# Merged and reordered stack loads, and joint maxima of two heads, in a two-layer decoder kernel

## The reference, cut to what matters

```python
x = _layernorm(x + L0_attn(x))            # a0: causal self-attention
x = _layernorm(x + L0_xattn(x, ctx))      # c0: cross-attention, 512 queries, 1024 keys
x = _layernorm(x + L0_ffn(x))             # soft mixture: 8 experts, 128 slots each
x = _layernorm(x + L1_attn(x))            # a1: causal
x = _layernorm(x + L1_xattn(x, ctx))      # c1: cross
x = _layernorm(x + L1_ffn(x))             # a2: pre-norm causal attention, then top-2 of 8 experts

# one attention, per batch and head:
att = softmax(q @ k.T / sqrt(16))         # causal layers mask the upper triangle
y   = att @ v                             # then an output projection
```

## Time and profile before

| | before |
|---|---|
| median of 3 runs | 3067.17 us (3059.79 to 3073.33) |
| the profiled execution | 3064.33 us |
| its span, first to last instruction | 3062.5 us |
| PE / DVE / ACT / POOL busy | 84% / 49% / 44% / 15% of the span |
| mean granted clock of PE | 0.916 of full speed |

### The profile page before, as it was taken

One profiled execution on the slowest core, in us unless ns is written; L12 is line 12 of the kernel. 1 busy time (PEld: TensorE's weight loads), 2 busy tenths in 40 slices (PEclk: granted clock), 3 DMA queues, 4 the chain that ended last, 5 costly groups with the idle time before them and its releaser, 6 DMA issues. The chain is left out here.

```text
span 3062.5 us, 48054 instructions
## 1 busy us (share of the span) xinstructions
PE 2568.9 (84%) x15793; PEld 1469.9 (48%) x15794; DVE 1499.4 (49%) x4196; ACT 1346.1 (44%) x2886; POOL 457.8 (15%) x719
## 2 busy tenths in 40 slices
PE   4999999999828979998588999898987986489992
PEld 2555544444314446676355544343434554356671
DVE  0555677888425420013444487777744564222223
ACT  2555456666634432211244456665754553022220
POOL 3222212101110000000112212212122000500004
PEclk7899999999969999999699999999998997599996
DMA  8344664454000012203644465354422332711102
GB/s 205 97 126 126 131 118 82 68 73 73 1 17 1 1 59 88 87 17 137 158 109 123 111 128 80 56 101 62 92 59 60 103 83 95 249 31 34 34 30 89
DMA packets 184550, 259.98 MB, mean 85 GB/s; under 512 B 32952, under 2 KB 106944, under 8 KB 184256
## 3 DMA queue, kind: packets, MB, share of 16 engines
q1 hardware_dynamic: 181264, 248.85, 34.5%
q0 software_dynamic: 3072, 8.39, 0.9%
HBM read 180.71 MB, written 81.53 MB: 86 GB/s over the span
## 5 line engine op out<-in xcount | busy, mean ns | idle before, releaser
L1345 ACT ACTIVATE second_p<-psum 128x512 f32<-128x512 f32 (+3 forms) x1024 | 461.7, 520 | 287.9 <-PE psum L1211 284.3
L1345 ACT ACTIVATE first_p<-psum 128x512 f32<-128x512 f32 (+3 forms) x768 | 365.7, 547 | 179.1 <-PE psum L1211 176.5
L1419 DVE TENSOR_REDUCE first_max_parts<-psum 128x1 f32<-128x512 f32 x512 | 323.0, 684 | 74.7 <-PE psum L1188 72.1
L1419 DVE TENSOR_REDUCE second_max_parts<-psum 128x1 f32<-128x512 f32 x512 | 321.9, 683 | 72.9 <-PE psum L1188 70.2
L1415 DVE CUSTOM_DVE_ANT_0 second_masked<-psum,mask_qk 128x384 f32<-128x384 f32 (+3 forms) x512 | 230.0, 489 | 230.7 <-PE psum L1188 189.1
L1201 PE MATMUL psum<-second_q,second_k 64*128 64x512 f32 (+3 forms) x1024 | 227.7, 440 | 42.1 <-DVE second_max_parts L1419 26.2
L1188 PE MATMUL psum<-second_k,second_q 64*128 64x512 f32 (+3 forms) x1024 | 203.7, 395 | 67.5 <-DMA second_k<-a_k_parts 51.5
L1223 PE MATMUL psum<-second_p,second_v_aug 128*32 128x512 f32 (+3 forms) x2048 | 240.1, 542 | 8.3 <-ACT second_p L1345 8.1
L1188 PE MATMUL psum<-first_k,first_q 64*128 64x512 f32 (+3 forms) x768 | 158.0, 411 | 61.7 <-ACT first_held L1382 26.0
L1201 PEld LDWEIGHTS psum<-second_q,second_k 64*128 64x128 f32 x1024 | 98.8, 188 | 230.1 <-issue 83.6
L1415 DVE CUSTOM_DVE_ANT_0 first_masked<-psum,mask_qk 128x128 f32<-128x128 f32 (+3 forms) x256 | 114.8, 488 | 179.7 <-PE psum L1188 152.5
(11 more groups left out here) (317 smaller groups left out, 3819.2 us busy)
## 6 DMA issues: line engine op xcount, KB each, us to landing
first_k<-c_k_parts SPq DMA_DIRECT2D x128, 128.0 KB, 5.7
second_q<-a_q_parts SPq DMA_DIRECT2D x256, 64.0 KB, 2.8
second_k<-a_k_parts SPq DMA_DIRECT2D x256, 64.0 KB, 2.9
second_k<-c_k_parts SPq DMA_DIRECT2D x128, 128.0 KB, 5.6
first_q<-a_q_parts SPq DMA_DIRECT2D x128, 64.0 KB, 2.9
first_k<-a_k_parts SPq DMA_DIRECT2D x128, 64.0 KB, 2.9
c_k_parts<-first_held SPq DMA_DIRECT2D x16, 512.0 KB, 3.2
first_q<-c_q_parts SPq DMA_DIRECT2D x128, 64.0 KB, 5.3
```

Source lines behind the costliest of these rows:

```text
L1345: evacuated(act.activation(probs[tile % 2][:, 2 * h + p, q0:SEQ], bank[:, q0:SEQ], ACT.Exp, scale=scale), event)
L1419: evacuated(v.reduce_max(max_parts[n % 2][:, h, p, qt, k0 // BANK:k0 // BANK + 1], bank[:, 0:width], axis=AX_X), event)
```

## The change

It has four parts.

**Loads.** A stack's q and k come in 8 transfers in place of 16. One transfer fills 32 partitions: for q the same 16 rows twice (a broadcast of the source), for k both parts. On the host the columns of the q and k weights are reordered (`by_heads`) so that the two pairs' rows of one `d` lie next to each other, and one row of a transfer is 2 x 512 (or 2 x 1024) numbers in one piece. In a causal layer the k rows now fill the first 1024 columns of the buffer, which `keys_of` unpacks.

**Order of the first loads.** The weights of later layers become an event of the list, behind the first stacks' loads. In the first stage a0's own weights still go ahead of everything; in the second stage, whose first projections are made elsewhere, all weights are in the event. The first two contexts are fetched some steps later, and the first stage's four first loads stand between its pieces.

**Maxima.** The shared banks become 0 to 6 and the sum's bank 7. In a cross layer, where a unit's two heads have neighbouring banks, one `reduce_max` over both writes two columns; where the ring wraps between them, two single ones stay.

**Experts.** `w_in` becomes `up_in` (first weight and its bias) and `down_in` (second weight and its bias); PE and ACT begin on the first, DVE and PE's second half wait for the second.

```diff
-SHARED_BANKS, PV_BANK = (0, 1, 2, 3, 4, 5, 7), 6
+SHARED_BANKS, PV_BANK = tuple(range(7)), 7
...
+        def keys_of(n):
+
+            keys = layer_of(n).keys
+            return ks[n % NB][:, :, :].rearrange("p i t -> p (i t)")[:, 0:2 * keys].rearrange("p (i t) -> p i t", i=2)
+
...
-                for dst, src, columns in own_loads:
-                    sp.dma_start(dst, src, allow_slow_non_contiguous=columns).then_inc(own_in, 16)
-                for dst, src, columns in later_loads:
-                    sp.dma_start(dst, src, allow_slow_non_contiguous=columns).then_inc(later_in, 16)
+                def fetch_weights(loads, done):
+                    for dst, src, columns in loads:
+                        sp.dma_start(dst, src, allow_slow_non_contiguous=columns).then_inc(done, 16)
+
+                if not layers[0].projected:
+                    fetch_weights(own_loads, own_in)
...
-                        for blk, (qp, kp) in enumerate(((0, 0), (0, 1), (1, 0), (1, 1))):
-                            at = slice(64 * h + HD * blk, 64 * h + HD * (blk + 1))
-                            sp.dma_start(qs[n % NB][at, :, :].bitcast(F32),
-                                         q_dram[qp, row:row + 2 * HD, :].rearrange("(i d) t -> d i t", d=HD)
+                        for half in range(2):
+                            at = slice(64 * h + 2 * HD * half, 64 * h + 2 * HD * (half + 1))
+                            sp.dma_start(qs[n % NB][at, :, :].bitcast(F32).rearrange("p i t -> p (i t)"),
+                                         q_dram[half, row:row + 2 * HD, :].rearrange("(d i) t -> d (i t)", i=2)
+                                         .unsqueeze(0).to_broadcast([2, HD, 2 * SEQ])
                                          ).then_inc(stack_in[n % NB], 16)
-                            sp.dma_start(ks[n % NB][at, :, 0:layer.keys].bitcast(F32),
-                                         k_dram[kp, row:row + 2 * HD, :].rearrange("(i d) t -> d i t", d=HD)
+                            sp.dma_start(ks[n % NB][at, :, :].rearrange("p i t -> p (i t)")[:, 0:2 * layer.keys].bitcast(F32),
+                                         k_dram[:, row:row + 2 * HD, :].rearrange("a (d i) t -> a d (i t)", i=2)
                                          ).then_inc(stack_in[n % NB], 16)
...
+                    elif event[0] == "weights":
+                        if layers[0].projected:
+                            fetch_weights(own_loads, own_in)
+                        fetch_weights(later_loads, later_in)
...
-                        pe.wait_ge(stack_in[r], 256 * (n // NB + 1))
+                        pe.wait_ge(stack_in[r], 128 * (n // NB + 1))
...
+                    low = bank_at[event, 0] % len(SHARED_BANKS)
+                    if not layer.causal and low + 1 < len(SHARED_BANKS):
+                        wait_full(v, event, 1)
+                        v.reduce_max(max_parts[n % 2][:, :, p, qt, k0 // BANK:k0 // BANK + 1],
+                                     c.psum[:, low:low + 2, 0:width], axis=AX_X).then_inc(ring_read["U"], 2)
+                        return
...
-        w_in = [c.sem(f"{name}_w_in{i}") for i in range(2)]
+        up_in, down_in = [c.sem(f"{name}_up_in{i}") for i in range(2)], [c.sem(f"{name}_down_in{i}") for i in range(2)]
...
-        pieces = {-3: front_pieces(a0, 0, "x") + FIRST_LOADS, -2: front_pieces(a0, 1, "x")}
+        pieces = {-3: front_pieces(a0, 0, "x") + FIRST_LOADS[:2],
+                  -2: front_pieces(a0, 1, "x") + FIRST_LOADS[2:5] + [("weights", 0, 0), ("load", 3, 0)]}
...
-        contexts = {-3: [("context", BATCH, 0), ("context", BATCH + 1, 0)]}
+        contexts = {-1: [("context", BATCH, 0), ("context", BATCH + 1, 0)]}
...
-        pieces = {-3: FIRST_LOADS}
-        contexts = {-3: [("context", BATCH, 0), ("context", BATCH + 1, 0)]}
+        pieces = {-3: FIRST_LOADS + [("weights", 0, 0)]}
+        contexts = {-2: [("context", BATCH, 0), ("context", BATCH + 1, 0)]}
...
+def by_heads(a, blocks):
+
+
+    own, rest = a[..., :blocks * D], a[..., blocks * D:]
+    own = own.reshape(own.shape[:-1] + (-1, 2, HD)).swapaxes(-2, -1).reshape(own.shape)
+    return np.concatenate([own, rest], axis=-1)
```

More of the change, by code:

```diff
@@ L1188, in unit @@
                         ins = pe.matmul(bank_of(event, h)[:, 0:width], qs[r][own, p, qt * P:(qt + 1) * P],
-                                        ks[r][own, p, k0:k0 + width], start=True, stop=True)
+                                        keys_of(n)[own, p, k0:k0 + width], start=True, stop=True)
                         filled(ins, event)
@@ L1200, in scores @@
                         own = slice(64 * h, 64 * h + 64)
-                        pe.matmul(bank_of(event, h)[:, q0:SEQ], ks[r][own, p, t * P:(t + 1) * P],
+                        pe.matmul(bank_of(event, h)[:, q0:SEQ], keys_of(n)[own, p, t * P:(t + 1) * P],
                                   qs[r][own, p, q0:SEQ], start=True, stop=False)
@@ L1563, in stage_experts @@
         hidden = sb("hidden", [P, HM, BANK])
-        w_in = [c.sem(f"{name}_w_in{i}") for i in range(2)]
+        up_in, down_in = [c.sem(f"{name}_up_in{i}") for i in range(2)], [c.sem(f"{name}_down_in{i}") for i in range(2)]
         s_up, s_gelu = c.sem(f"{name}_up"), c.sem(f"{name}_gelu")
         s_down, s_read = c.sem(f"{name}_down"), c.sem(f"{name}_read")
-        per_load = 16 * 4
+        per_load = 16 * 2
         tiles = BANK // P
@@ L1584, in body @@
                     one = bass.ds(e, 1)
-                    sp.dma_start(up[r][:, :, :], w1[one, :, :].rearrange("o (k p) n -> p (o k) n", p=P)).then_inc(w_in[r], 16)
-                    sp.dma_start(up_bias[r][:, :], b1[one, :, :].rearrange("o p m -> p (o m)")).then_inc(w_in[r], 16)
-                    sp.dma_start(down[r][:, :, :], w2[one, :, :].rearrange("o (m p) n -> p (o m) n", p=P)).then_inc(w_in[r], 16)
+                    sp.dma_start(up[r][:, :, :], w1[one, :, :].rearrange("o (k p) n -> p (o k) n", p=P)).then_inc(up_in[r], 16)
+                    sp.dma_start(up_bias[r][:, :], b1[one, :, :].rearrange("o p m -> p (o m)")).then_inc(up_in[r], 16)
+                    sp.dma_start(down[r][:, :, :], w2[one, :, :].rearrange("o (m p) n -> p (o m) n", p=P)).then_inc(down_in[r], 16)
                     wait_for(sp, s_read, tiles * (e - 1))
                     sp.dma_start(down_bias[r][:, :], b2[one, :].rearrange("o n -> (o n)").partition_broadcast(P)
-                                 ).then_inc(w_in[r], 16)
+                                 ).then_inc(down_in[r], 16)
                 for_experts(sp, body)
@@ L1596, in body @@
                 def body(e, pair, r):
-                    pe.wait_ge(w_in[r], (pair + 1) * per_load)
+                    pe.wait_ge(up_in[r], (pair + 1) * per_load)
                     for m in range(HM):
@@ L1603, in body @@
                         ins.then_inc(s_up, 1)
+                    pe.wait_ge(down_in[r], (pair + 1) * per_load)
                     for t in range(tiles):
@@ L1617, in body @@
                 def body(e, pair, r):
-                    act.wait_ge(w_in[r], (pair + 1) * per_load)
+                    act.wait_ge(up_in[r], (pair + 1) * per_load)
                     wait_for(act, s_down, e * tiles)
@@ L1629, in body @@
                 def body(e, pair, r):
-                    v.wait_ge(w_in[r], (pair + 1) * per_load)
+                    v.wait_ge(down_in[r], (pair + 1) * per_load)
                     for t in range(tiles):
@@ L2289, in by_groups @@
     return np.concatenate([others, own], axis=-1)
+HEADED = {"L0_attn_w_attn": 2, "L0_attn_b_attn": 2, "L1_attn_w_qkv": 2}
+HEADED.update({f"{layer}_{x}": 1 for layer, names in (("L0_xattn", ("Wq", "Wk", "bq", "bk")), ("L1_xattn", ("wq", "wk", "bq", "bk")),
+                                                      ("L1_ffn", ("Wq", "Wk", "bq", "bk"))) for x in names})
+def by_heads(a, blocks):
+    own, rest = a[..., :blocks * D], a[..., blocks * D:]
+    own = own.reshape(own.shape[:-1] + (-1, 2, HD)).swapaxes(-2, -1).reshape(own.shape)
+    return np.concatenate([own, rest], axis=-1)
 def kernel(**inputs):
@@ L2303 @@
             a = by_groups(a, name in TURNED_ROWS)
+        if name in HEADED:
+            a = by_heads(a, HEADED[name])
         if name == "ctx_768":
```

## The result

The changed kernel takes 3903.8 us (3900.75 to 3909.94), 1.2726 times the time of before (95% interval 1.2691 to 1.2761): 837 us slower. The forecast was 3985 in a range of 3300 to 4300. The profiled execution has a span of 3903.4 us, 841 over that of before. All times are medians of executions at the usual pace; one execution of the run split16, at 5426 us, was far slower than its four others and is left out.

A forecast was written before the change was run, and what follows sets the result against it. PE, busy 84% of the span, bounded the kernel; with the change, each turn becomes gap plus load. Loops, starts, experts and clock: 381 + 418 + 56 - 4 + 70 = +921 on 3064.3, about 3985 us; range 3300 to 4300.

The forecast's parts named there:

- The mechanism: Loop over stacks: two DMA engines carry each load, issued only after its predecessor's first use; each turn is gap plus load.
- causal load: q and k of a causal stack: 0.524 MB per engine at 25.0 GB/s plus latency and values, 24 us.
- cross load: q and k of a cross stack: 0.786 MB per engine at 25.0 GB/s plus latency and values, 34.7 us.
- gaps: From a stack's first unit to the next load's first issue: 203 us in 28 turns, 205 in 44, kept as before.
- first loop: First stage, 28 turns of gap plus load: 1046 us where the windows had 665, +381.
- second loop: Second stage, 44 turns of gap plus load: 1432 us where the windows had 1014, +418.
- start of the first stage: First four stacks' loads: the fourth stack's unit comes at about 131 us in place of 106, +25.
- between the loops: Second stage's fourth stack comes at 1540 us, not 1509, +31; experts' first matmul waits for two transfers only, -4.
- The clock: PE idles in every turn, so the gap's matmuls start at the 1.2 GHz level: 1 us a turn, +70.
- The joint reduce: Merged maxima on VectorE: 1225 ns each, 63 us saved but hidden under load waits, 0; uncovered, at most 26.2 us.
- Rival 1: Loads: sixteen engines serve the new form too, a load lasts 6.6 us, total about 2950 us; chance 0.10.
- line of about 5 engines: Rival 1's threshold: with more than about 5 engines a load, 8.4 plus 2.9 us, is under the old load.

The follow-up runs named there:

- split16: The changed kernel with each load split in two: 16 transfers of 16 partitions a stack, no broadcast, source rows walked as 16; 3041 us, 0.9906 of before.
- lead16_single: lead16 with the joint maxima of two heads undone, so every reduce takes one bank; 2954.7 us, 0.963 of before.
- lead16: The changed kernel with the two leading dimensions of each load's source swapped, 16 rows first, then the 2 copies or parts; 2957.8 us, 0.9642 of before.
- split8: split16 with the 16 rows of each transfer's source walked as 8 x 2; 3179.8 us.

## Why the prediction was right

**The mechanism** was right: two engines a transfer, loads that follow their predecessor's first unit, and a load of q and k that ends last in 65 of the 72 turns. The prediction had it so in every turn; in seven turns of the second stage the stack had landed before PE came to it. PE's waits (803 us, over 600 forecast), its share in the windows (63 to 73%, under 75) and the DMA share (0.15 to 0.23) are as foretold. Two signs did not come as named: the page gives no landing for these loads, so the turn's 22.9 us stands in its place, and single gaps are longer than 2 to 8 us (the first is 10.45). The Trainium skill's rule that the number of engines is the largest up to 16 that divides the slowest dimension of both patterns (DMA: Bandwidth & Descriptors, "Why a DMA increments its semaphore by 16 and not by 1") agrees with the trace at 2 and 4, by the shares 0.13 and 0.25; which two engines serve, no run here shows.

**The terms**, forecast and measured, where a loop's time is its windows above (28 and 44 turns, whose gaps and loads are summed from the timeline as in the turn above, a load up to its stack's first unit; the first gap stands below):

| term | forecast | measured |
|---|---|---|
| causal load, first / second stage | 24 | 23.3 / 24.5 |
| cross load, first / second stage | 34.7 | 32.9 / 33.4 |
| gaps, first + second stage | 203 + 205, and 70 for the clock | 199 + 227 |
| first loop | +381 | +340 |
| second loop | +418 | +433 |
| start of the first stage | +25 | +25.5 |
| between the loops (experts, second start) | +31 - 4 | +38 |
| end | 0 | +4 |
| sum | +921 | +841 |

```profile
131.49 0.47 PE L1200 MATMUL psum<-first_k,first_q 64*128 64x128 f32 x2 [11.21 <-DMA first_k<-a_k_parts]
...
141.94 0.66 SPq L1036 DMA_DIRECT2D first_q<-a_q_parts  x1
```

The gap of the turn in a2, before and after, as windows (columns of the earlier trace rows):

```profile
2426.80:2428.90 2.10, 2.10 (x30) 1.45 (x26) 1.72 (x13) 1.83 (x4) 0.74 (x1) 1.00 0.00 0
```

```profile
3231.46:3234.00 2.54, 2.54 (x20) 1.84 (x22) 0.51 (x4) 0.60 (x1) 0.73 (x1) 0.50 0.03 6
```

Two terms were mis-sized. **The clock** (+70): the granted clock did fall, to 0.76 to 0.84 over a layer's window. In the gap shown, after 10.96 us of waiting, it is 0.50, the 1.2 GHz level, where it was 1.00, and the first unit takes 0.47 us where the earlier trace rows has 0.22. But this gap grew by only 0.45 us, all 72 grew by 17 us together, and those of the first stage not at all; slow matmuls outside a gap run while a load is awaited. **The load** was 44 us too long over all turns (2070 forecast, 2026 measured): its two engines move 26 GB/s each and not 25.0. Between the loops, PE's wait at the experts did fall by 3.8 us (12.4 to 8.6), but the time up to the second stage's first load fell by under 1 us beyond the 14 of the moved weights. The second start itself cost 39 us and not 31: from the first issue to the fourth stack's unit 96 us pass, where the sum had 88:

```profile
1816.68 0.66 SPq L1036 DMA_DIRECT2D second_q<-a_q_parts  x1
...
1912.48 0.25 PE L1200 MATMUL psum<-second_k,second_q 64*128 64x128 f32 x2
```

**The joint reduce** takes 1223 ns, as the 1225 of the earlier trace rows said:

```profile
L1425 DVE TENSOR_REDUCE first_max_parts<-psum 128x2 f32<-128x1024 f32 x222 | 268.0, 1223 | 231.1 <-PE psum L1200 231.0
```

The 26.2 us that bounded its worth without cover were no measure of it: most of that wait was POOL's, not VectorE's, and lead16_single shows a worth of nothing.

**Rival 1** had the right sum for another kernel: 2950 for sixteen engines, and with 16 rows first it is 2958. That the sums agree is in part luck: its 26 us for maxima came to nothing, while the cross layers, which it had at none, gave 19. Its line of about 5 engines doesn't hold either: 8.4 plus 2.9 is 11.3 us, not under the old load's 11.2. So the merging is good in itself, and only the order of two dimensions turned 109 us of gain into 837 of loss. Of the versions run, lead16 and lead16_single (2958 and 2955) are the fastest, both under the kernel before.

## What to carry to other kernels

When transfers are merged, put the dimension that 16 divides first at both ends, a broadcast or a number of parts behind it; where the buffer's rows are only summed over, their nesting is free. A DMA share stuck at 2/16 or 4/16 while an engine waits for transfers points to the fault. Follow a wait for an engine one link further before pricing a faster instruction: the engine may itself have stood idle for a third.

## What the runs showed of the hardware

- An issue cost SP more in the runs where the patterns of source and destination differ in form: 0.59 us in the merged loads and 0.65 with 8 x 2 rows, against 0.42 where both ends are alike. This is most of what makes split8 slower than split16. Why it depends on the form is open.
- Wide stores landed later among narrow loads. The 512 KB stores of c0's keys, themselves unchanged, land 15.4 us after issue in the changed kernel, 3.2 before and 3.1 in lead16. Not every store does: those of c1's keys land after 3.4 (3.1 before). That the two busy engines also carry a part of each store fits this, and wasn't tested. The rows of the profile, before, after and in lead16 (count, KB, us to landing):

```profile
c_k_parts<-first_held SPq DMA_DIRECT2D x16, 512.0 KB, 3.2
```

```profile
c_k_parts<-first_held SPq DMA_DIRECT2D x16, 512.0 KB, 15.4
```

```profile
c_k_parts<-first_held SPq DMA_DIRECT2D x16, 512.0 KB, 3.1
```
